# Equal cells merged within four tiles of 128 edges: count scatters and feature gathers issued in runs of four

## The reference

```python
# block 0: messages along the edges, summed at idx_i, then a residual MLP
g   = einsum('pr,fr->pf', f_ij, W_att)           # edge_attr (100000 x 16)
x_i = ssp(xa @ W_i.T + b_i);  x_j = ssp(xa @ W_j.T + b_j)
msg = x_j[idx_j] * g
m   = x_i + segment_sum(msg, idx_i)
...
# block 1: two layers of attention over the same edges, 2 heads of 64
alpha = einsum('ehc,ehc->eh', q[dst], k[src]) / 8
ex    = exp(alpha - segment_max(alpha, dst)[dst])
a     = ex / segment_sum(ex, dst)[dst]
out   = segment_sum(a[:, :, None] * v[src], dst).mean(axis=1) + x @ ws + bs
```

## Time and profile before

| | us |
|---|---|
| median of the three runs shown | 3809.78 |
| lowest, highest run | 3809.74, 3824.54 |
| span of the profiled execution | 3811.1 |
| POOL busy in it | 2877.6 (76%) |
| PE busy | 3035.6 (80%) |
| DVE busy | 2605.0 (68%) |
| ACT busy | 714.9 (19%) |

### The profile page before, as it was taken

One profiled execution on the slowest core, in us unless ns is written; L12 is line 12 of the kernel. 1 busy time (PEld: TensorE's weight loads), 2 busy tenths in 40 slices (PEclk: granted clock), 3 DMA queues, 4 the chain that ended last, 5 costly groups with the idle time before them and its releaser, 6 DMA issues.

```text
span 3811.1 us, 56791 instructions
## 1 busy us (share of the span) xinstructions
PE 3035.6 (80%) x18659; PEld 1691.1 (44%) x18659; DVE 2605.0 (68%) x8565; ACT 714.9 (19%) x895; POOL 2877.6 (76%) x1959
## 2 busy tenths in 40 slices
PE   4877787787787787787787787786688888899996
PEld 3555555555555555555555555553222222322222
DVE  4667666667666666666666666665777776688786
ACT  2000000000000000000000000004355554343343
POOL 3588888888888888888888888884288887587784
PEclk7988988988988888898898898897799999899998
DMA  8511111111111111111111111111644454233320
GB/s 310 159 13 12 13 13 13 13 13 13 13 13 13 13 13 12 13 13 13 13 13 13 12 13 13 12 11 1 165 142 142 145 149 119 59 83 83 83 71 9
DMA packets 244258, 194.38 MB, mean 51 GB/s; under 512 B 146300, under 2 KB 224981, under 8 KB 244181
## 3 DMA queue, kind: packets, MB, share of 16 engines
q1 hardware_dynamic: 86035, 159.92, 14.1%
q0 software_dynamic: 137984, 26.19, 11.9%
q10 hardware_dynamic: 20162, 7.27, 1.0%
HBM read 112.79 MB, written 80.42 MB: 51 GB/s over the span
## 4 chain that ended last, share of the span: by engine, by line
POOL 39%; issue 23%; PE 19%; DMA 10%; DVE 6%; ACT 3%; POOLq 1%; DVEq 0%; SPq 0%
POOL edge_counts L428 17%; POOL nodes_and_gaps L419 16%; DMA edge_counts<-small 9%; PE PS L1228 6%; PE PS L1251 5%; POOL scores L482 4%; PE PS L1260 3%; PE PS L1133 2%; POOL counts_and_logs L465 1%; DVE scores L978 1%; DVE PS L989 1%; DVE counts_and_logs L964 1%; PE PS L1240 1%; ACT scores L655 1%; PE PS L1234 1%
## 5 line engine op out<-in xcount | busy, mean ns | idle before, releaser
L1133 PE MATMUL PS<-scores 128*128 128x320 bf16 x11760 | 1847.5, 322 | 528.2 <-DVE scores L844 528.2
L1133 PEld LDWEIGHTS PS<-scores 128*128 128x128 bf16 x11760 | 1226.1, 105 | 1161.6 <-DVE scores L844 537.9
L428 POOL DMA_INDIRECT edge_counts<-small x752 | 1207.9, 1606 | 263.5 <-issue 229.3
L419 POOL DMA_INDIRECT nodes_and_gaps<-xj_rows,small x784 | 799.3, 1020 | 290.8 <-issue 192.3
L482 POOL TENSOR_TENSOR scores<-scores,max_of_targets 125x896 f32<-125x896 f32 x335 | 701.1, 2133 | 190.6 <-ACT max_of_targets L650 142.5
L805 DVE SCALAR_TENSOR_TENSOR scores<-PS,small,scores 128x256 bf16<-128x256 f32 x784 | 332.7, 480 | 671.9 <-PE PS L1113 524.6
L844 DVE TENSOR_SCALAR scores<-scores,small 128x192 bf16<-128x192 bf16 x3920 | 745.9, 296 | 7.6 <-issue 4.0
L978 DVE TENSOR_TENSOR scores<-PS,counts_and_logs 125x896 f32<-125x896 f32 x350 | 377.6, 1082 | 201.9 <-PE PS L1228 74.3
L1228 PE MATMUL PS<-q_features,k_features 64*125 64x448 f32 x1400 | 369.3, 608 | 71.3 <-DVE scores L978 68.6
L655 ACT ACTIVATE scores<-scores 125x896 f32<-125x896 f32 x350 | 329.9, 948 | 371.2 <-POOL scores L482 364.3
L1251 PE MATMUL PS<-scores,v_nodes 125*64 125x448 f32 x1400 | 347.6, 581 | 43.2 <-ACT scores L655 38.8
(11 more groups left out here) (171 smaller groups left out, 1755.3 us busy)
## 6 DMA issues: line engine op xcount, KB each, us to landing
counts_and_logs<-edge_counts SPq DMA_DIRECT2D x70, 980.0 KB
edge_counts<-counts_and_logs SPq DMA_DIRECT2D x50, 766.0 KB
edge_counts<-counts_and_logs SPq DMA_DIRECT2D x35, 980.0 KB
nodes_and_gaps<-xj_rows,small POOLq DMA_INDIRECT x784
edge_counts<-small POOLq DMA_INDIRECT x752
counts_and_logs<-edge_counts SPq DMA_DIRECT2D x70, 113.8 KB
scores<-in_edge_attr_dram ACTq DMA_DIRECT2D x95, 48.0 KB
edge_counts<-counts_and_logs SPq DMA_DIRECT2D x35, 113.8 KB
```

The source lines that it names most:

```text
L419: pool.indirect_dma_start(gx[u][:, s * F:(s + 1) * F], None, xj_dram, bass.IndirectOffsetOnAxis(ap=dcur[u][:, s:s + 1], axis=0)).then_inc( ...
L428: pool.indirect_dma_start(cnt_dram, bass.IndirectOffsetOnAxis(ap=index[:, s:s + 1], axis=0), value[:, s:s + 1], None, compute_op=ALU.add). ...
L1133: ins = nc.tensor.matmul(PS[:, b, 0:HI * F], onehot[:, s, b * P:b * P + 128], spread[:, s, i].rearrange("p h f -> p (h f)"), start=first a ...
```

## The change

A constant `ROUND` = 4 takes the place of the 2: equal cells are merged within four tiles, POOL issues four scatters and then four gathers, twice in a group, and waits for earlier scatters once for each four. The numbers of scatters, gathers and matmuls stay. Each L805 now covers all 512 columns of the bank. The pattern `low` grows from 384 to 896 columns and moves to the tensor `h_features`, which is free at that time; `lowh`, `ranked`, and the trash cells grow as well.

```diff
-FILL = -(-(N * ND + 2 * EP) // (128 * FILLS))
+ROUND = 4
+FILL = -(-(N * ND + ROUND * EP) // (128 * FILLS))
...
-EARLIER = 4 * EP
+EARLIER = 2 * ROUND * EP
...
-        low = taken(3 * EP)
-        lowh = taken16(3 * EP, bf16)
-        ranked = taken16(G * 2 * EP, bf16).rearrange("p (s c) -> p s c", s=G)
+        low = hTt[:, HC:HC + (2 * ROUND - 1) * EP]
+        lowh = taken16((2 * ROUND - 1) * EP, bf16)
+        ranked = taken16(G * ROUND * EP, bf16).rearrange("p (s c) -> p s c", s=G)
...
-                if s % 2 == 0:
+                if s % ROUND == 0:
                     pool.wait_ge(sem("count_added"), 16 * G * h + 16 * s)
...
-                for s in range(0, G, 2):
+                for s in range(0, G, ROUND):
                     if scatters:
-                        for e in range(2):
+                        for e in range(ROUND):
                             scatter(g - BEHIND, s + e, cidx[u], cnt[u])
-                    for e in range(2):
+                    for e in range(ROUND):
                         gather(g, u, s + e)
...
-                for e in range(2):
-                    link(nc.vector.tensor_scalar(trash_all[:, e:EJ:2], key_all[:, e:EJ:2], -1.0, trash[:, e:e + 1], ALU.mult, ALU.add))
+                for e in range(ROUND):
+                    link(nc.vector.tensor_scalar(trash_all[:, e:EJ:ROUND], key_all[:, e:EJ:ROUND], -1.0, trash[:, e:e + 1], ALU.mult, ALU.add))
...
-                    nc.vector.scalar_tensor_tensor(ranked[:, s, :], PS[:, 5, 2 * EP * pair:2 * EP * pair + 2 * EP], keyc[:, s:s + 1],
-                                                   lowh[:, EP * (1 - e):EP * (3 - e)], ALU.is_equal, ALU.mult, accum_out=weight[:, s:s + 1]
-                                                   ).then_inc(sem("matched"), 1)
+                    nc.vector.scalar_tensor_tensor(ranked[:, s, :], PS[:, 5, 0:ROUND * EP], keyc[:, s:s + 1],
+                                                   lowh[:, EP * (ROUND - 1 - e):EP * (2 * ROUND - 1 - e)], ALU.is_equal, ALU.mult,
+                                                   accum_out=weight[:, s:s + 1]).then_inc(sem("matched"), 1)
```

More of the change, by code:

```diff
@@ L183, in build @@
         srch_all, dsth_all = taken16(EJ, f16), taken16(EJ, f16)
-        assert at[0] <= 25000, at[0]
+        assert at[0] <= SLOTS * HEADS * D, at[0]
         srcf_all, dstf_all = cnt_all, trash_all
@@ L198, in build @@
         cnt = [col(G) for _ in range(2)]
-        trash_i = col(2).bitcast(i32)
-        trash = col(2)
+        trash_i = col(ROUND).bitcast(i32)
+        trash = col(ROUND)
         srch, dsth = kh[:, 0:G], kh[:, G:2 * G]
@@ L407, in _ @@
             pool.wait_ge(sem("low_set"), 1)
-            nc.gpsimd.affine_select(out=low, in_=low, compare_op=ALU.is_gt, fill=1.0, base=EP,
-                                    pattern=[[-1, 3 * EP]], channel_multiplier=1).then_inc(sem("low_ready"), 1)
-            nc.gpsimd.iota(trash_i, pattern=[[EP, 2]], base=N * ND, channel_multiplier=1).then_inc(sem("trash_iota"), 1)
+            nc.gpsimd.affine_select(out=low, in_=low, compare_op=ALU.is_gt, fill=1.0, base=(ROUND - 1) * EP,
+                                    pattern=[[-1, (2 * ROUND - 1) * EP]], channel_multiplier=1).then_inc(sem("low_ready"), 1)
+            nc.gpsimd.iota(trash_i, pattern=[[EP, ROUND]], base=N * ND, channel_multiplier=1).then_inc(sem("trash_iota"), 1)
             def settled():
@@ L801, in dedupe @@
                 for s in range(G):
-                    if s % 4 == 0:
-                        dve.wait_ge(sem("keys_in_psum"), 2 * g + s // 4 + 1)
-                    pair, e = s // 2 % 2, s % 2
-                    nc.vector.scalar_tensor_tensor(ranked[:, s, :], PS[:, 5, 2 * EP * pair:2 * EP * pair + 2 * EP], keyc[:, s:s + 1],
-                                                   lowh[:, EP * (1 - e):EP * (3 - e)], ALU.is_equal, ALU.mult, accum_out=weight[:, s:s + 1]
-                                                   ).then_inc(sem("matched"), 1)
+                    e = s % ROUND
+                    if e == 0:
+                        dve.wait_ge(sem("keys_in_psum"), 2 * g + s // ROUND + 1)
+                    nc.vector.scalar_tensor_tensor(ranked[:, s, :], PS[:, 5, 0:ROUND * EP], keyc[:, s:s + 1],
+                                                   lowh[:, EP * (ROUND - 1 - e):EP * (2 * ROUND - 1 - e)], ALU.is_equal, ALU.mult,
+                                                   accum_out=weight[:, s:s + 1]).then_inc(sem("matched"), 1)
                 dve.wait_ge(sem("matched"), G * (g + 1))
```

## The result

The changed kernel takes **3786.61 us** (median of 5, 3786.41 to 3789.88), beside 3809.74 for the kernel before in the same call: ratio 0.9938, 95% interval 0.992 to 0.9956. The forecast was 3811, no change.

A forecast was written before the change was run, and what follows sets the result against it. POOL was taken as the bound by one microsecond, 25.88 us a group against 24.82 for the ring. Waits of -98.7 and matches of +99.5 made +0.8: 3811.1 to 3811.9, less 1.3 gives 3810.6, called 3811; range 3781 to 3846.

The forecast's parts named there:

- POOL, fewer waits: POOL's loop: two of four waits in a group go; they cost nothing before, so the gain is 0.
- POOL, longer runs: POOL's loop: third and fourth DMAs of each run get shorter, 0.38 us less a group, POOL's beat 25.50.
- DVE, wider matches: DVE's eight matches a group: 0.27 us more each; only the last four are in the ring, 1.07 a group.
- The bound changes hands: Edge-stage loop: L827's waits go nearly to zero, POOL waits for staged counts, its gain is spent; +0.8 us in all.
- the ring: DVE and PE's loop: product, spreads, sums, last keys, last matches, next product; 24.82 us a group if gathers were always there.
- The ring at 25.89: Loop of DVE and PE after the change: grows from 24.82 to 25.89 us a group (25.65 by the lower match price).
- PE's stretch: PE's first 45 matmuls of a group, after idle, partly at the lower clock: 8.3 us in the mean.
- rival C: PE's slow stretch after idle grows to 8.71 us in each group: 37 us slower, 3848 us; chance 0.20.
- Rival B: POOL stays the bound with shorter runs, matches costing less in the ring: 3775 at full gain, 3789 by lower price; chance 0.17.
- idle time costs twice: PE's clock: by this rule a wider match would cost its 1.07 us and a slower stretch behind it.
- Start and tail: Before POOL's first scatter: 0, at most +5 us; after the loop, last scatters some 16 us earlier: 0, at best -1.5.

The follow-up runs named there:

- e5: Changed kernel with PE making the second four tiles' keys one tile earlier, after tile 4 and not 5: 3775.55 us, ratio 0.9846.
- e12: The edit of e5 on the changed kernel once more, in another call beside the changed kernel: 3775.7 us, ratio 0.9893.
- e0: The changed kernel itself, repeated without an edit in another call on another chip: ratio 0.9984, beat 26.05 us.
- e6: Changed kernel with eight one-column memsets on DVE behind the last four matches: ratio 1.0011, beat 26.13 us.
- e3: Kernel before, 256-column matches, with two of each eight scatters left out (tiles 3 and 7): 3656.78 us, ratio 0.9551.
- e4: Changed kernel, 512-column matches, with two of each eight scatters left out (tiles 3 and 7): 3786.38 us, ratio 0.9886.
- e11: Changed kernel with 24 more PE matmuls of 320 columns at each group's end, into PSUM columns nobody reads: 3783.45 us, ratio 0.9914.
- e10: e4 with one 512-column memset more on DVE behind the wait for the last matches: 3823.78 us, ratio 1.0031.
- e2b: Kernel before with POOL's scatters and gathers in runs of four, 256-column matches, all counts sent to trash cells: ratio 1.1196.

## Why the prediction was wrong

**POOL, fewer waits: 0. Right.** The waits were free, as the 0.30 us brackets said; the brackets after are the same.

**POOL, longer runs: 0.38 us a group, beat 25.50. Right.** 25.51 and 25.49 where POOL bounds (e5, e12). The busy sum of one undisturbed group was 20.38 in the prediction; the eight DMAs of the round above, twice, are 20.40. The mean group has more, 21.00 before and 20.61 in e12, by the DMAs that meet DVE.

**DVE, wider matches: 0.27 each, half of them beside PE. Right.** They start 0.67 us apart, from the last keys to the end of the fourth match it is 1.07 us more, and the first four did not show.

**The bound changes hands: half right.** The waits of L827 went from 103.2 to 1.1. But POOL was to run ahead and wait for the staged counts, so that its gain was spent there, and in the changed kernel it never did. Its busy time is 21.00 us a group before, 20.76 in the changed kernel and 20.61 in e12. Of the 0.39 that the longer runs save, 0.15 went into DMAs that became longer where they meet DVE, and 0.24 is the gain. POOL and the ring ran side by side at one beat, neither waiting for the other. Only in the call of e0 and e6 did POOL wait as forecast.

**The ring at 25.89: wrong, and this is the step that failed.** I took the ring's length as the paced beat less the mean wait, 24.82, and added 1.07. The runs have 24.28 for the ring alone at 256 columns (e3) and 25.60 at 512 (e4). The subtraction treats PE's stretch of 8.2 as fixed. It is not: it depends on where in it the clock comes back to its higher level, and the ring's other parts set when PE starts. In the trace after it is 8.03, 0.17 less; from product to spread 0.03 less, and the copies behind the last match 0.05 less. Together this is the 0.25 that separates 25.89 from 25.64, 23 us over the stage. Nor does the ring of e3 give the result: the wait of 1.06 was not the whole slack, but adding 1.07 to 24.28 gives 25.35, wrong the other way, where 25.60 was measured, with a PE stretch 0.40 longer. No sum of fixed parts gives both. The rows for it were there: the earlier trace rows had 8.71 behind 5.61 of idle and 6.29 behind 2.98, and rival C used them, but only for the worse.

**Rival B, given a chance of 0.17, is what the time looks like, but not how it came about.** B has 3789 for a cheaper match, and the time is 3787, but the match cost what was said, and the ring gave back elsewhere; that the two times are near each other is chance. The full gain of B, 3775, is what e5 and e12 reach.

**The Trainium skill's rule** (TensorE: Matmul & The Clock Gate, Part 1: The HAM clock gate), that activity releases the slow level: e11 agrees, 24 matmuls in the idle shortened PE's stretch by 1.1 us in the mean. What the prediction drew from it, that idle time costs twice, is no rule that one can sum with here: 7.67 us behind 5.55 of idle, 9.04 behind 4.74 (e4).

**Rival C, slower.** It did not come. The nearest is the beat of 26.05 in one call of four, and not by C's mechanism: PE's stretch is 8.22 there, for 8.20 in the kernel before, while POOL stands at the end of its lead and product to spread is longer (4.82). The ratio was still 0.9984; the kernel before read 3833 in that call, and no trace shows why. (The prediction works out 3848 for C and takes 3846 for the end of its range; nothing hangs on it.)

**Start and tail: 0. Right.** The first product comes 3.1 us later, POOL's first scatter at 135.19 (134.66 before), which fits `counts_cleared` as its gate. After the last product 0.7 us less; the last scatter starts at 2620.63 where it started at 2661.43, 41 us earlier: 22 from the stage, and the rest since behind the last gathers POOL waits some 2.2 us once for four scatters and no longer once for two. As forecast, none of the latter reached the span.

**What stays open.** What picks the beat of the changed kernel (25.6 to 25.7 three times, 26.05 once) was not settled: the two differ in POOL's distance to DVE, at most 4 us or some 13, but no run set that distance on purpose. In the faster beat POOL, which can do 25.5, is slowed by its meetings with DVE to just the ring's beat; what keeps them together at 3.4 us was not tested. That the 51.2 us for two groups come from PE's clock is supported by the falls of the clock in e10, 51.20 us apart, and by the half of each delay that comes back; no run took the falls away altogether (e11 did in half of the groups, and its pairs stayed near 51.2). And POOL's order alone, with real cells and narrow matches, was not tried, since two adds to one cell could be in flight.

## What to carry to other kernels

When two loops are within a few per cent, don't take the slack of the second as its mean wait. PE's stretch at the lower clock changes with the moment at which it starts, from 7.67 to 9.04 us in one trace (e4), and the means over a loop by up to 0.4 in a group of 25. Give such a sum an error of some tenths of a microsecond a group on both sides. Check too whether the loop that lost the bound really waits. And if a change makes the runner-up the bound, look at once for the step that can be moved off its ring: here one line, the keys one tile earlier, was worth 12 us beside the changed kernel in the same call.

## What the runs showed of the hardware

- A ring of DVE and PE with 5 us of PE idle in each round kept a beat of 51.20 us for two groups (the same to 0.01 in the rows of e10) in 28 of 46 pairs though 0.29 us of work had been added to it, and slipped from it in the others.
- PE's granted clock fell 0.56 us before a group's first sum in e4 and 0.76 us before it in e10, and the 45 matmuls took 7.67 and 7.57 us: half of the delay came back. With 1.17 and 1.57 us they took 9.04 and 8.84.
- The time of an indirect DMA on POOL depends on what stood before it: a gather 1.01, 0.98, 0.94, 0.94 and an adding scatter 1.62, 1.58, 1.57, 1.56 in a run, and 0.30 of idle before each. Beside DVE's one-hot rows a scatter took 1.94.
- Scatters that add to the same 1024 neighbouring cells in every group (e2b) land too late for the four gathers behind them to cover: 183 waits of up to 5.1 us, 533.7 in all.
- Small DVE instructions behind an instruction with an accumulated output, and ahead of the wait for it, cost nothing here: from the last match to the next product it is 2.47 us with eight memsets of one column and without them (e6, e0).
